# Reordering the last batch of an attention stage by head groups

## The reference

```python
def _L1_xattn_ref(q, k, v):            # q = layernorm(x), k = v = ctx_2048; (b, 256, 512)
    qh = q.reshape(b * 8, 32, m); kh = k.reshape(b * 8, 32, -1); vh = v.reshape(b * 8, 32, -1)
    qk = jnp.einsum('bdm,bdn->bmn', qh, kh) / sqrt(32)
    sm = jax.nn.softmax(qk, axis=-1)
    return jnp.einsum('bmn,bcn->bcm', sm, vh).reshape(b, c, m)

x = x + tanh(g_xattn[0]) * _L0_xattn_ref(_layernorm(x), ctx, ctx, ...)   # retention-like mixing
x = x + tanh(g_ffn[0])   * _L0_ffn_ref(_layernorm(x), ...)               # dense feed-forward
x = x + tanh(g_xattn[1]) * _L1_xattn_ref(_layernorm(x), ctx, ctx)
x = x + tanh(g_ffn[1])   * _L1_ffn_ref(_layernorm(x), ...)               # shared part + top 6 of 64
```

## Time and profile before

| | |
|---|---|
| timed runs | 1054.55, 1055.43, 1059.3 us; median 1055.43 |
| profiled execution | 1064.39 us, span 1062.7 us, mean granted TensorE clock 0.983 |
| TensorE busy | 995.9 us (94%) |
| VectorE busy | 600.4 us (57%) |
| ScalarE busy | 333.7 us (31%) |
| GpSimd busy | 465.1 us (44%) |
| DMA | 262.23 MB, mean 247 GB/s |

### The profile page before, as it was taken

How to read it: one execution, slowest core, us unless ns; L and a number is a source line. 1 busy time by engine, 2 the same in 40 slices (tenths; PEclk the granted TensorE clock), 3 DMA queues, 4 the chain that set the end, 5 groups by cost and what they waited for, 6 DMA issues and landing times.

```text
span 1062.7 us, 15353 instructions
## 1 busy us (share of the span) xinstructions
PE 995.9 (94%) x5629; PEld 609.4 (57%) x5630; DVE 600.4 (57%) x1249; ACT 333.7 (31%) x491; POOL 465.1 (44%) x457
## 2 busy tenths in 40 slices
PE   7999899999999999999999998767999999998986
PEld 6986444554564564564555453227777777775532
DVE  3333454765765855756756847443546555552566
ACT  3411023224133233323233231432434444442121
POOL 1000024625657467577568435442255555556000
PEclk9999899999999999999999999978999999999899
DMA  8892269598681590780610509336899999965998
GB/s 309 293 393 108 82 228 348 206 360 311 237 307 45 199 340 1 232 306 8 232 63 31 181 5 400 154 145 238 307 363 380 376 372 370 370 254 210 367 417 322
DMA packets 93622, 262.23 MB, mean 247 GB/s; under 512 B 10454, under 2 KB 10582, under 8 KB 92784
## 3 DMA queue, kind: packets, MB, share of 16 engines
q1 hardware_dynamic: 43760, 146.18, 37.7%
q10 hardware_dynamic: 31872, 63.97, 16.1%
q0 software_dynamic: 17920, 51.15, 12.2%
HBM read 129.91 MB, written 139.72 MB: 254 GB/s over the span
## 4 chain that ended last, share of the span: by engine, by line
PE 71%; DVE 8%; POOL 7%; DMA 5%; issue 4%; ACT 3%; another core or an unknown queue 2%; POOLq 0%; ACTq 0%; SPq 0%; DVEq 0%
PE banks L1266 17%; PE banks L1861 10%; PE banks L1276 9%; PE banks L1850 6%; PE banks L1870 6%; POOL t_psum L766 5%; PE banks L1364 5%; PE banks L1426 4%; DMA e_eo<-y_d 4%; DVE t_nmx L1057 2%; PE banks L1444 2%; ACT t_probs L857 2%; PE banks L396 1%; PE banks L402 1%
## 5 line engine op out<-in xcount | busy, mean ns | idle before, releaser
L1684 POOL DMA_INDIRECT y_d<-e_eo,e_ids x128 | 124.5, 972 | 127.2 <-DVE e_eo L1781 93.9
L1057 DVE TENSOR_REDUCE t_nmx<-banks 128x4 f32<-128x2048 f32 x56 | 128.1, 2287 | 60.9 <-PE banks L1364 60.9
L766 POOL TENSOR_TENSOR t_psum<-t_psum,t_probs 128x512 f32<-128x512 f32 x104 | 128.6, 1268 | 62.1 <-ACT t_probs L857 61.3
L857 ACT ACTIVATE t_probs<-banks 128x2048 f32<-128x2048 f32 x56 | 105.1, 1878 | 141.7 <-PE banks L1429 117.8
L778 POOL DMA_INDIRECT xs_d<-r_norm,r_xaddr x96 | 96.0, 1000 | 49.5 <-issue 25.0
L1426 PE MATMUL banks<-b_qry,b_key 32*128 32x512 f32 x512 | 73.5, 643 | 11.7 <-ACT t_probs L857 5.7
L736 POOL TENSOR_TENSOR f_rstd<-f_veps,mhalf 128x2 f32<-128x2 f32 x24 | 16.8, 700 | 149.3 <-DVE f_veps L955 149.3
L1850 PEld LDWEIGHTS banks<-ident,e_xg 128*128 128x128 f32 x512 | 57.1, 143 | 26.6 <-issue 25.7
L766 POOL TENSOR_TENSOR t_psum<-t_probs,t_probs 128x512 f32<-128x512 f32 x52 | 66.5, 1316 | 12.1 <-DVE b_qry L1047 6.0
L1364 PE MATMUL banks<-b_key,b_qry 32*128 32x512 f32 x448 | 64.8, 648 | 7.0 <-DVE t_nmx L1057 5.2
L1850 PE MATMUL banks<-ident,e_xg 128*128 128x128 f32 x512 | 64.5, 281 | 4.5 <-DMA e_xg<-xs_d 4.1
(11 more groups left out here) (223 smaller groups left out, 1643.4 us busy)
## 6 DMA issues: line engine op xcount, KB each, us to landing
xs_d<-zero ACTq DMA_DIRECT2D x32, 1056.0 KB, 7.1
e_xg<-xs_d SPq DMA_DIRECT2D x32, 1056.0 KB
y_d<-zero ACTq DMA_DIRECT2D x24, 1024.0 KB
e_xg<-y_d SPq DMA_DIRECT2D x16, 768.0 KB, 11.2
e_eo<-y_d SPq DMA_DIRECT2D x16, 768.0 KB, 13.4
wo<-in_wud SPq DMA_DIRECT2D x6, 768.0 KB
wupT<-in_wud SPq DMA_DIRECT2D x6, 768.0 KB
a_x<-in_x SPq DMA_DIRECT2D x8, 512.0 KB, 4.7
```

Source lines behind the costliest of these rows:

```text
L766: ins = g_.tensor_tensor(psum0[:, q, :], first[:, q, :], probs[s % NP][:, q, :], ALU.add)
L857: A(probs[s % NP][:, :, :], quad[:, :, :], ACT.Exp, scale=SCALE1).then_inc(W["exp_ok"], 1)
L1057: V.tensor_reduce(nmx[g][:, m, :], quad[:, :, :], axis=AX.X, op=ALU.max, negate=True).then_inc(W["mx_ok"], 1)
L1684: g_.indirect_dma_start(out=y_d, out_offset=bass.IndirectOffsetOnAxis(ap=ids[:, HC * p + n:HC * p + n + 1], axis=0), in_=eo[u][:, n, :], i ...
```

## The change

`ENDING` is rewritten from `T.A0/6` on. Group 0 of batch 7 is taken through maxima, parts and row (`L.S0` to `L.S3`, `L.P0`, `L.M0`) and starts its Q steps; group 1's maxima, now eight halved pieces `L.S4a` to `L.S7b` in the two lent banks, stand between the Q and V steps of group 0. `L.M0` uses work bank 0, one of the lent pair, and `L.S4a` waits until it is copied. Group 0's sums in batch 7 go to GpSimd (`L.sum0a`, b, c) and `L.Z0`; `L.V0` to `L.V3` lose their extra matmuls. `L.Z0` stands ahead of `L.Q4`. A new step `L.K1` takes the copy of batch 6's group 1, which now comes after the copy of group 0's row. On SyncE three of the six pair loads stay at `F.down1`; the other three and the accumulator load move behind `T.cT/7` (`L.more`). `L.up0` is one step again and stands with `L.up1` between `L.V7` and `L.turn1`. The scatters `R.x1/6` to `R.x3/6` now stand behind `L.stats0`, and all of tile 0's scatters (`L.rows0a`, b) behind `L.stats1`.

```diff
-... T.A0/6 L.V4/6 L.V5/6 T.add0/6 R.x0/5 L.S0/7 L.S1a/7
-L.V6/6 L.V7/6 T.cT/7 T.A1/6 L.S1b/7 L.S2/7 L.up0a/7 T.add1/6 R.x1/5 L.S3a/7 L.S4/7 L.S3b/7 L.up0b/7 L.P0/7 R.x2/5 R.stats/6 L.S5/7 L.S6a/7 L.M0/7 L.up0c/7 L.up0d/7
-R.norm/6 L.S7/7 L.S6b/7 R.turnA/6 R.turnB/6 R.x3/5 R.acc/5 R.acc/6 L.P1/7 L.Q0/7 R.gates/6 R.keep/6 L.Q1/7 L.V0/7 R.top/6 L.Q2/7 L.M1/7 R.pos/6 L.V1/7 L.Q3/7
-R.slots/6 R.x0/6 R.weigh/6 L.V2/7 R.x1/6 R.x2/6 L.Q4/7 L.V3/7 L.A0/7 L.add0/7 L.stats0/7 R.x3/6 L.Q5/7 L.V4/7 L.norm0/7 L.Q6/7 L.V5/7 L.turn0/7 L.Q7/7 L.gates0/7 L.top0/7
-L.V6/7 L.pos0/7 L.slots0/7 L.rows0a/7 L.V7/7 L.A1/7 L.add1/7 L.stats1/7 L.rows0b/7 L.norm1/7 L.turn1/7 L.gates1/7 L.top1/7 L.pos1/7 L.slots1/7 L.rows1/7
-L.weigh0/7 L.weigh1/7 L.up1/7 L.up2/7 L.up3/7 F.next/7
+... T.A0/6 L.V4/6 L.S0/7 L.S1a/7 T.add0/6 R.x0/5 L.V5/6 L.S2/7 L.S1b/7
+L.V6/6 R.x1/5 L.S3/7 L.V7/6 T.cT/7 L.more/7 L.P0/7 L.M0/7 L.K1/6 L.Q0/7 T.A1/6 L.S4a/7 R.x2/5 T.add1/6 L.S4b/7 L.Q1/7 L.V0/7 R.x3/5 R.stats/6 L.S5a/7
+L.sum0a/7 L.Q2/7 L.S5b/7 L.V1/7 R.norm/6 L.S6a/7 L.sum0b/7 L.Q3/7 R.turnA/6 L.S6b/7 L.V2/7 L.S7a/7 L.sum0c/7 R.turnB/6 L.V3/7 L.S7b/7 R.gates/6
+R.acc/5 R.acc/6 R.keep/6 L.P1/7 L.M1/7 R.top/6 L.Z0/7 L.Q4/7 R.pos/6 R.slots/6 R.x0/6 L.A0/7 R.weigh/6 L.add0/7 L.stats0/7 R.x1/6 L.Q5/7 L.V4/7 L.norm0/7
+R.x2/6 L.Q6/7 L.V5/7 L.turn0/7 L.Q7/7 L.gates0/7 L.top0/7 L.V6/7 R.x3/6 L.pos0/7 L.slots0/7 L.V7/7 L.up0/7 L.A1/7 L.up1/7 L.add1/7 L.stats1/7 L.rows0a/7
+L.rows0b/7 L.norm1/7 L.turn1/7 L.gates1/7 L.top1/7 L.pos1/7 L.slots1/7 L.rows1/7 L.weigh0/7 L.weigh1/7 L.up2/7 L.up3/7 F.next/7
...
-CHOSEN = {("L.V4", 6): 2, ("L.up0a", 7): 3, ("L.M0", 7): 2, ("R.turnA", 6): 3, ("R.turnB", 6): 2}
+CHOSEN = {("L.V4", 6): 2, ("L.M0", 7): 0, ("R.turnA", 6): 2, ("R.turnB", 6): 2, ("R.gates", 6): 2}
...
+def nth_sum(b, g):
+    return 2 * b + g - (b == LB)
+def by_pool(b, g):
+    return g == 0 or b < LB - 1
...
         def last_exps(n):
             def stage(b):
                 act.wait_ge(W["pv_mm"], 8 * b - NP + n + 1)
+                if n >= KC:
+                    act.wait_ge(W["sum_ok"], 3 * nth_sum(b, 0) + (1, 1, 2, 3)[n - KC])
                 act.wait_ge(W["st_mm"], 8 * b + n + 1)
...
+                if name == "L.S4a":
+                    pe.wait_ge(W["mrow_ok"], 2 * b + 1)
...
+        stages["L.Z0"] = sums(0)
         for n in range(KC * NG):
-            stages[f"L.V{n}"] = last_weighted(n)
+            stages[f"L.V{n}"] = last_weighted(n) if n >= KC else weighted(n)
```

More of the change, by code:

```diff
@@ L469 @@
     "R.turnA": ("x4T_ok", 2, 1), "R.turnB": ("x4T_ok", 2, 2), "R.gates": ("mark_ok", 1, 1), "R.pos": ("route_ok", 1, 1),
[1 row of a table removed]
[1 row of a table added]
     "L.turn0": ("x4T_ok", 2, 1), "L.turn1": ("x4T_ok", 2, 2), "L.gates0": ("mark_ok", 1, 1), "L.gates1": ("mark_ok", 1, 2),
[1 row of a table removed]
[1 row of a table added]
 } | {f"L.up{c}": ("raw_ok", 0, c + 1) for c in range(len(UPS))}
-RELEASES["L.up0a"] = RELEASES.pop("L.up0")
 PIECES = {name: (i, n, slice(2 * half, 2 * half + 2) if halved else slice(0, G), halved) for i, (name, n, half, halved) in enumerate((
-    ("L.S0", 0, 0, False), ("L.S1a", 1, 0, True), ("L.S1b", 1, 1, True), ("L.S2", 2, 0, False), ("L.S3a", 3, 0, True), ("L.S4", 4, 0, False),
-    ("L.S3b", 3, 1, True), ("L.S5", 5, 0, False), ("L.S6a", 6, 0, True), ("L.S7", 7, 0, False), ("L.S6b", 6, 1, True)))}
-CHOSEN = {("L.V4", 6): 2, ("L.up0a", 7): 3, ("L.M0", 7): 2, ("R.turnA", 6): 3, ("R.turnB", 6): 2}
+    ("L.S0", 0, 0, False), ("L.S1a", 1, 0, True), ("L.S2", 2, 0, False), ("L.S1b", 1, 1, True), ("L.S3", 3, 0, False),
+    *((f"L.S{n}{'ab'[half]}", n, half, True) for n in range(KC, 2 * KC) for half in range(2))))}
+CHOSEN = {("L.V4", 6): 2, ("L.M0", 7): 0, ("R.turnA", 6): 2, ("R.turnB", 6): 2, ("R.gates", 6): 2}
 QUADS = {f"{p}.{u}{n}": (s, n + 1) for u, s in (("S", "mx_ok"), ("Q", "exp_ok")) for n in range(8) for p in "TL" if p + u != "LS"}
@@ L505, in occupants @@
             lent = True
-        elif name == "L.S6b":
+        elif name == "L.S7b":
             holder[0:2] = [(name, b)] * 2
@@ L687, in first_pairs, with pairs_ahead @@
                 sp.wait_ge(W[n], 2 * NB)
+            pairs_ahead(0, 3)
+        def pairs_ahead(first, end):
             wu, wd, both = pair_weights(v)
-            for p in range(len(wu)):
+            for p in range(first, end):
                 load_pair(sp, io, both, w_in, p)
@@ L697, in loads_ahead, with more_ahead @@
                 first_pairs()
-                for u in range(2):
-                    sp.wait_ge(W[f"accst{u}"], 16 * 2)
-                early_acc(0, 4)
+        def more_ahead(b):
+            pairs_ahead(3, 6)
+            for u in range(2):
+                sp.wait_ge(W[f"accst{u}"], 16 * 2)
+            early_acc(0, 4)
         def r_acc(b):
@@ L714, in shared_rows @@
                 sp.dma_start(nrT[k][:, :, :], nrT_d[c, :, :].rearrange("p (k s) -> p k s", k=KC)).then_inc(W["nr_in"], 16)
-        steps({"F.keys": f_keys, "F.down1": loads_ahead, "T.cT": t_values, "F.next": f_next, "R.acc": r_acc, "R.keep": r_keep, "L.load": shared_rows})
+        steps({"F.keys": f_keys, "F.down1": loads_ahead, "L.more": more_ahead, "T.cT": t_values, "F.next": f_next, "R.acc": r_acc, "R.keep": r_keep, "L.load": shared_rows})
         sp.wait_ge(W["pv_mm"], 8 * NB)
@@ L757, in stage @@
                 if n == 1:
-                    since(pool, W["z_mm"], 2 * b + g)
+                    since(pool, W["z_mm"], nth_sum(b, g))
                     first = probs[(s - 1) % NP]
@@ L913, in scalar @@
                   "R.turnA": r_turn(0), "R.turnB": r_turn(1), "R.pos": r_exps(None),
-                  "L.M0": rows_of(0), "L.M1": rows_of(1), "L.V3": keep(0), "L.V7": keep(1)}
+                  "L.M0": rows_of(0), "L.M1": rows_of(1), "L.V3": keep(0), "L.K1": keep(1),
+                  "L.V7": lambda b: keep(1)(b) if b == LB else None}
         for t in range(T):
@@ L928, in stage @@
                 act.wait_ge(W["su_mm"], c + 1)
-                A(raw[c], bank(f"L.up{c}" if c else "L.up0a", b)[:, :], ACT.Copy).then_inc(W["raw_ok"], 1)
+                A(raw[c], bank(f"L.up{c}", b)[:, :], ACT.Copy).then_inc(W["raw_ok"], 1)
             return stage
         for c in range(len(UPS)):
-            stages[f"L.up{c}" if c else "L.up0d"] = shared_raw(c)
+            stages[f"L.up{c}"] = shared_raw(c)
         steps(stages)
@@ L1070, in stage @@
             def stage(b):
[L1071 removed]
+                dve.wait_ge(W["mx_ok"], 8 * b + (KC * (g + 1) if b < LB else (5, 13)[g]))
                 dve.wait_ge(W["zero_ok"], 1)
```

43 lines of the change are left out of this document (13 added, 30 removed), and 4 rows, old and new, of the table RELEASES.

## The result

The change makes the kernel slower. Its median is 1063.07 us in 20 executions (1052.3 to 1067.23), against 1056.53 us in 20 of the kernel before, run beside it (1053.8 to 1063.35): a ratio of 1.0058, 95% interval 1.0042 to 1.0074. Forecast were 1051.9 us and a range up to 1060.0. The profiled execution took 1064.88 us (span 1063.1).

The account below looks back on a forecast made before the run. Handoffs, not TensorE's work, were taken to bound the rewritten stretch, up to the first last-tile scatter. That scatter comes 3.7 us earlier, less 0.2 for the experts' start: 1055.43 - 3.5 = 1051.9 us, range 1045.5 to 1060.

Parts of the forecast that it names:

- The walk: Step-by-step timing of the new order from `L.V4/6` on: Q4 at 681.2, first `L.rows1` scatter at 711.0.
- Second group beside the rounds: Half pieces S4a to S7b between Q and V steps: 5.0 us per pair, Q4 could start at 680.6.
- the tail: V7's end to first `L.rows1` scatter: gates at full clock, GpSimd decides, 13.1 us; scatter at 711.0 against 714.7.
- rival A: GpSimd's sums too slow at `L.Z0` ahead of `L.Q4`: 1.72 us per addition, clock halves, 1060 us; chance 0.17.
- R.stats and R.norm of batch 6, 1.8 and 1.0 on VectorE, lie in there: Both operations fit on VectorE before the last half maxima end at 678.15.
- Q4 released by the row copy later than 682.5: Sign that dearer half-piece handoffs, not the forecast, hold: Q4 waits for M1's row copy past 682.5.
- Pieces pace the rounds: In the second group, a pair of half pieces takes about 5.0 us against 3.4 of a round.
- Q4 released by Z0 and GpSimd: GpSimd's three sums end at 680.4, Z0 at 681.2, releasing Q4 then, against 684.56 before.
- The values' load: `T.cT`, issued at 653.5 and needed by V0 at 662.7, takes 5 us and is hidden.
- The disturbance of 7.7 us: Extra waiting between Q4's start and V7's end in the old profile, taken as absent from timed runs.
- rival C: The waits around Q4 belong to the old order and vanish with it: 11.4 us gained, 1044 us; chance 0.13.
- Rival B: Half pieces through two banks each cost 0.4 us more, Q4 3.2 later, no gain: 1055 us; chance 0.20.

Follow-up runs that it names:

- s2_split: Changed kernel with `L.up0` in four quarters, two ahead of `L.M0`, two ahead of `L.Q0`, and `L.up1`, `L.up2` behind V7: 1054.3 us, ratio 0.9991.
- e4_before_nofill: Kernel before, with the four quarters of `L.up0` moved from between its maxima to the end, ahead of `L.up1`: 1070.89 us, ratio 1.0042.
- quiet sets: Two sets of runs without unexplained waits between 640 and 740 us; the kernel before took 1057.27 and 1055.7 us in them.
- b0_before: Kernel before, unchanged, timed and profiled again: 1057.86 us, ratio 0.9991.
- set 5: Changed kernel and two versions with `L.up0` split into quarters, one also keeping `R.norm` off GpSimd's sums; kernel before 1055.7 us, ratios 1.0037, 0.9991, 1.0012.
- e9_tail: Kernel before with only the new tail: `L.up1`, `L.up2` behind V7, all rows0 scatters behind the statistics: 1065.33 us, ratio 0.9997.

## Why the prediction was wrong

The walk's moments beside the changed kernel and beside s2_split, which is the changed order with its clock held (us from the span's start):

```
                                forecast   changed   s2_split
Q0 starts                        656.6     656.77    657.10
exp0, exp1 start                 658.0, 662.7   659.39, 666.71   658.56, 663.02
exp2, exp3 start                 666.1, 670.6   671.59, 676.50   666.41, 671.08
GpSimd's three sums end          680.4     684.1     680.9
last half maxima (S7b) end       678.15    689.3     680.8
Q4 starts                        681.2     692.80    683.33
V7 ends                          697.9     711.6     700.15
first rows1 scatter              711.0     724.92    713.48
experts' first transpose         725.2     739.16    727.88
span                             1051.5    1063.1    1053.3
```

**The step that failed** is the one called "Second group beside the rounds", in the prices that it used: it took 1.13 us for each half piece and 1.3 to 1.46 for each Q, which are rows at full clock, for a stretch in which the change takes away TensorE's work. The prediction thought of the clock for the tail and for the experts' start, and in rival A only behind a late GpSimd. It did not ask what the clock would do in the 2.7 us of idle time that its own walk put just ahead of Q0 (V7/6 to 653.45, Q0 at 656.6). At 0.50 a Q takes 2.09 us and a piece of four matmuls 1.92; the exponentials come 1.4, 4.0, 5.5 and 5.9 us late, and Q4 11.6, of which some 2 are the second term below. The Trainium skill, TensorE: Matmul & The Clock Gate (Why this matters for your kernels), warns of idle gaps between bursts. The trace agrees in kind, with 0.50 for 12 us and more behind gaps of 2.05 and 0.69, but each of these is shorter than the gaps that the page names, so here the measurement decides. I cited that section for the wrong place.

What shows that this is the cause: taking the same work out of the old order gives the same loss (e4_before_nofill, 1.0042). Putting it back into the new one takes the loss away in both quiet sets, 1.0041 to 1.0000 and 1.0037 to 0.9991. With the clock at 1.00 the exponentials start within 0.6 us of the walk, and the changed kernel's two executions with a clock of 0.989 and 0.990 took 1052.3 and 1051.57 us. What is not shown: in the other kind of set the same edit gained nothing in three comparisons (1.0068 to 1.0099, and, with the contention removed, 1.0032 to 1.0042 and 1.0039 to 1.0041). There S3's late release lengthens the very gap, and the late release near V7 costs 4.4 to 5.3 us more, which no filling touches.

**A second term was left out**: "R.stats and R.norm of batch 6, 1.8 and 1.0 on VectorE, lie in there". Beside GpSimd's additions `R.norm` and its token addition take 3.1 to 4.1 us from the first start to the last end, instead of 1.1. In s2_split they delay the maxima of S6a, which start 4.56 us behind those of S5b (667.48 and 672.04) where the undisturbed pace is 2.45, so 2.1 us. That is most of the 2.7 us by which the last maxima end late (680.8 for 678.15); Q4 misses the walk by 2.1, since the walk had 0.6 of waiting for GpSimd there. The Trainium skill's sentence, GPSIMD Engine Reference, Key points (shared SBUF interfaces, contention), was in the prediction, but I applied it to GpSimd's side only. There the rows were right: 4.93 to 5.28 us for a sum, so 1.23 to 1.32 per addition, and rival A's 1.72 never came. It is VectorE that pays.

**The base was mixed.** The kernel before also loses its clock between 656 and 669 in part of its executions (b0_before). With a clock of 0.990 or 0.991 it takes 1053.2 to 1054.0 us in set 5, and I subtracted from a median of 1055.43. So even the one execution of the change that holds its clock there gains about 2 us (1051.57 against 1053.2 to 1054.0), not 3.5, and the ten of s2_split at 0.987 to 0.992 gain nothing (1053.0 to 1055.1). That 1051.9 was met by two executions is therefore partly luck, of two errors that cancel: the base was 1.4 to 2.2 us too high, and the contention, about 2 us, was left out. No trace of those two executions is kept, so how they spend their time is not shown.

Point by point: Q0 at 656.6 was right. "Pieces pace the rounds" was right: at full clock the half maxima stand 2.45 us apart (S6a to S7a in s2_split: 672.04, 674.49, 676.94), as walked. "Q4 released by Z0 and GpSimd" was right in Z0 and wrong in GpSimd: in every trace of the new order Z0 starts right behind M1 (the last maxima's row) and Q4 right behind Z0, and GpSimd's sums were done 1.1 us or more before. The values' load was hidden: V0 starts right behind Q1 in the changed kernel (666.54) and in s2_split (662.86). 16.7 from Q4 to V7's end was right where the clock held (700.15-683.33 = 16.8), and 18.8 in the changed kernel, where it was at 0.50 from 690.7 to 694.1 and from 697.5 to 700.9. The tail was right: 13.3 instead of 13.1 behind V7, 14.2 more to the first transpose (739.16-724.92). That it should gain anything is not borne out (e9_tail, 0.9997), since the quiet old tail takes 13.4. The disturbance of 7.7 us was treated rightly: the old order has it in some executions and not in others, and rival C falls. Rival B, dearer handoffs of the half pieces, falls, since at full clock they keep the walk. Its sign, Q4 released by the row copy later than 682.5, came by half: Q4 started at 692.80, but the copy was done at 691.64, under Z0, and what was slower were matmuls.

**Open.** What the late releases are. They stand at S3's maxima (3.7 to 5.9 us) and again near V7 (3.3 to 6.3 us) in the new order, and around Q4 and V3 in the old one (11.2 to 11.3 us), in all traces of three sets (two chips) and in none of the two quiet ones (two more chips), with TensorE's records complete long before. The first profile of the kernel before has the one around Q4 too (11.41 us), though the 20 executions beside it are as short as those of the quiet sets and the changed kernel's profile there has none; if that profile is of the same chip, which the record doesn't say, it is not the chip alone. The cause can't be told from these runs. Nor did any order hold its clock in all executions: s2_split has two of twelve at 1058 or more. No version beats the kernel before by a measurable amount.

## What to carry to other kernels

When an edit shortens a waiting chain by moving TensorE's independent work out of it, price the matmuls that remain at both clocks and look for the first gap in front of them; work that is "free to move" may be what holds the clock. Price an operation on VectorE that reads and writes SBUF beside a stream of GpSimd additions at two to seven times its row, however short it is. And read the mean clock of each execution beside its time before taking a median as the base: here one median covered two groups 4 us apart, more than the whole forecast gain of 3.5.
